# A 1444-key attention whose slots take in the value projection, the feed-forward and the norms behind it

## The reference

```python
z = self_attn(x, Wq1, Wk1, Wv1);            x = layer_norm(x + z, ln1_g, ln1_b)
z = cross_attn(x, context, Wq2, Wk2, Wv2);  x = layer_norm(x + z, ln2_g, ln2_b)
z = relu(x @ fc1_w + fc1_b) @ fc2_w + fc2_b
return layer_norm(x + z, ln3_g, ln3_b)
# the caller: x = x + tanh(g) * that, then x = x + tanh(g') * ffn(layernorm(x))
```

## Time and profile before

| | us |
|---|---|
| median of 3 runs | 2369.92 (2368.28 to 2373.06) |
| the profiled execution | 2365.66 |
| its span, first to last instruction | 2363.8 |
| cross-attention, first score matmul to last result copy | 134.8 to 402.2 |
| tail of stage A, to the first instruction of stage B | 402.2 to 624.4 |

### The profile page before, as it was taken

One profiled execution on the slowest core, in us unless ns is written; L12 is line 12 of the kernel. 1 busy time (PEld: TensorE's weight loads), 2 busy tenths in 40 slices (PEclk: granted clock), 3 DMA queues, 4 the chain that ended last, 5 costly groups with the idle time before them and its releaser, 6 DMA issues. The chain is left out here.

```text
span 2363.8 us, 43064 instructions
## 1 busy us (share of the span) xinstructions
PE 2000.1 (85%) x16906; PEld 1274.0 (54%) x16906; DVE 1588.6 (67%) x3726; ACT 1324.0 (56%) x2169; POOL 547.8 (23%) x476
## 2 busy tenths in 40 slices
PE   3779997465499999999999999999997788888997
PEld 2546665343255565555565565655654456565554
DVE  4835453688478778788788887887882466655554
ACT  3645554466236666666566666666665455544444
POOL 1410000454212222222221221222221232311122
PEclk9779998666579999999999999999999788877999
DMA  5026663000123232232232231332320100201431
GB/s 159 1 76 190 187 181 95 1 18 21 60 89 112 78 106 99 80 117 94 85 117 79 101 119 62 115 109 70 117 97 20 57 15 10 35 1 31 90 64 42
DMA packets 120022, 189.25 MB, mean 80 GB/s; under 512 B 36770, under 2 KB 94090, under 8 KB 118414
## 3 DMA queue, kind: packets, MB, share of 16 engines
q1 hardware_dynamic: 119822, 186.50, 25.6%
HBM read 103.33 MB, written 11.76 MB: 49 GB/s over the span
## 5 line engine op out<-in xcount | busy, mean ns | idle before, releaser
L1409 DVE TENSOR_REDUCE b_part_max<-psum 128x1 f32<-128x482 f32 (+3 forms) x1248 | 737.3, 650 | 187.6 <-PE psum L1286 173.5
L1199 ACT ACTIVATE b_PT<-psum 128x800 f32<-128x800 f32 x768 | 616.4, 836 | 386.0 <-PE psum L1305 379.6
L1286 PE MATMUL psum<-b_KH,b_QBD 64*128 64x482 f32 (+1 forms) x1152 | 421.4, 442 | 46.3 <-DVE b_part_max L1409 43.4
L1305 PE MATMUL psum<-b_QS,b_KS 64*128 64x200 f32 x3072 | 438.6, 288 | 0.5 <-ACT b_PT L1199 0.3
L1305 PEld LDWEIGHTS psum<-b_QS,b_KS 64*128 64x128 f32 x3072 | 339.6, 187 | 16.2 <-issue 11.8
L1321 PE MATMUL psum<-b_PT,b_V 128*32 128x200 f32 x6144 | 341.1, 339 | 0.6 <-ACT b_PT L1199 0.6
L1286 PEld LDWEIGHTS psum<-b_KH,b_QBD 64*128 64x128 f32 x1152 | 196.6, 188 | 198.0 <-DVE b_part_max L1409 118.6
L1122 POOL TENSOR_TENSOR b_KL<-b_KF,b_KH 128x1444 fp32r<-128x1444 f32 x32 | 106.9, 3340 | 691.9 <-PE psum L1305 669.7
L1321 PEld LDWEIGHTS psum<-b_PT,b_V 128*32 128x32 f32 x6144 | 159.9, 109 | 149.0 <-ACT b_PT L1199 82.3
L385 POOL TENSOR_TENSOR a_rs<-a_ve,a_half 100x4 f32<-100x4 f32 x48 | 50.0, 1041 | 419.5 <-DVE a_ve L758 419.4
L1709 ACT ACTIVATE c_HE<-psum,C 128x400 f32<-128x400 f32 x128 | 75.5, 594 | 94.7 <-PE psum L1925 90.1
(11 more groups left out here) (275 smaller groups left out, 3133.0 us busy)
## 6 DMA issues: line engine op xcount, KB each, us to landing
b_KS<-b_KH SPq DMA_DIRECT2D x64, 722.0 KB
a_CT<-in_ctxt SPq DMA_DIRECT2D x32, 722.0 KB, 4.2
b_CT<-in_ctxt SPq DMA_DIRECT2D x32, 722.0 KB, 4.3
b_KS<-b_KL SPq DMA_DIRECT2D x32, 722.0 KB
a_CN<-in_ctxn SPq DMA_DIRECT2D x32, 704.0 KB
att_scratch<-b_AO SPq DMA_DIRECT2D x32, 200.0 KB, 1.9
c_G<-gates_scratch SPq DMA_DIRECT2D x4, 1600.0 KB
c_KBD<-gates_scratch SPq DMA_DIRECT2D x4, 1600.0 KB
```

Source lines behind the costliest of these rows:

```text
L1199: nc.scalar.activation(PT[:, kt % 2, 2 * a:2 * a + 2, :], psum[:, 2 * a:2 * a + 2, 0:TG], ACT.Exp).then_inc(sem["pt_ready"], 1)
L1286: m = mm(bank(b, D, size), QBD[rows, j % 2, tile * D:(tile + 1) * D], KH[rows, j % 2, at_:at_ + size], start=True, stop=True)
L1305: m = mm(bank(p, D, 2 * T, (s % 2) * 2 * T), KS[rows, j % 2, s, kt * D:(kt + 1) * D], QS[rows, j % 2, s * 2 * T:(s + 1) * 2 * T], start=Tr ...
L1409: v.tensor_reduce(part_max[0:rows, q, c:c + 1], bank(b, rows, CHUNKS[c][1]), AX.X, ALU.max)\
```

## The change

- The front steps, `values2` to norm 4, are set in slots s. Slot s below 32 is sequence s of the attention; each tick of the tail stands for two more slots. Unit u does the step of lag k in slot 4 (u + 1) + k. Their PSUM bank is 5 in the attention and 1 in the tail.
- The scores are 512, 512 and 422 keys wide. Even sequences use banks 0, 1, 2, odd ones 2, 3, 4. The part in the shared bank 2 (part 2) is computed at the start of a slot, the two others of sequence m+2 between the second and third transposes of m; the wait for the key load stands in front of part 0.
- The mask of m+1 stands ahead of the whole weighing of m. The result copy on ACT stands behind the exponential of the next sequence.
- The residual is kept in `XIN` and the normalised rows in `Y`, for all units; `X` and its four buffers are gone. GpSimd computes `YB` ahead of the norm's shift.
- The tail has 11 ticks instead of 12. The loads of the context and their buffers are not touched.

```diff
+        def due(s, lag):
+            u, rest = divmod(s - lag, GROUP)
+            return u - 1 if rest == 0 and 1 <= u <= UNITS else None
+        def hop(s, rows, cols):
+            return bank(5 if s < BATCH else 1, rows, cols)
+        def chunks(m):
+            parts = [(c, 2 * (m % 2) + c, min(512, SPAD - 512 * c)) for c in range(3)]
+            return parts if m % 2 == 0 else parts[1:] + parts[:1]
...
# POOL
+            def front(s):
+                for lag, step in ((1, rstd(2)), (6, rstd(3)), (2, gain2), (7, gain3), (8, rstd(4))):
+                    if due(s, lag) is not None:
+                        step(due(s, lag))
...
# ACT
             for m in range(BATCH):
+                front_start(m)          # lag 4: turned2
                 keep(m, 0)
-                keep(m, 1)
                 if m + 1 < BATCH:
                     cut_row(m + 1)
+                keep(m, 1)
                 keep(m, 2)
-                act.wait_ge(sem["z2T_psum"], m + 1)
-                nc.scalar.copy(RT[:, m // GROUP, t.ts_(m % GROUP)], bank(7, D, T, TG)).then_inc(sem["z2T_ready"], 1)
+                front_middle(m)         # lag 4: rectify; 9, 2, 7: norms 4, 2, 3
                 if m + 1 < BATCH:
                     probabilities(m + 1)
+                result(m)
...
# PE
+            def score(m, part):
+                u, j = divmod(m, GROUP)
+                c, b, size = chunks(m)[part]
+                if part == 0:
+                    if m < 2:
+                        pe.wait_ge(sem["rT2_ready"], UNITS)
+                    else:
+                        pe.wait_ge(sem["e2_ready"], m - 1)
+                    pe.wait_ge(ct_loaded[m % 3], (m // 3 + 1) * 16)
+                if part == 2 and m:
+                    pe.wait_ge(sem["e2_ready"], m)
+                mm(bank(b, T, size), RT[:, u, t.ts_(j)], CT[:, m % 3, 512 * c:512 * c + size],
+                   start=True, stop=True).then_inc(sem["s2_psum"], 1)
...
             for m in range(BATCH):
+                pe.wait_ge(sem["e2_ready"], m + 1)
                 if m + 1 < BATCH:
-                    scores(m + 1)
-                pe.wait_ge(sem["e2_ready"], m + 1)
...
+                    score(m + 1, 2)
+                turn_keys(m, 0)
+                turn_keys(m, 1)
+                first_hop(m)            # lag 4: hidden
+                if m + 2 < BATCH:
+                    score(m + 2, 0)
+                    score(m + 2, 1)
+                turn_keys(m, 2)
+                if m + 1 < BATCH:
+                    cut(m + 1)
                 pe.wait_ge(cn_loaded[m % 3], (m // 3 + 1) * 32)
                 pe.wait_ge(sem["pT_ready"], m * 3 + 2)
                 weigh(m, 0, 8)
-                if m + 1 < BATCH:
-                    cut(m + 1)
                 pe.wait_ge(sem["pT_ready"], m * 3 + 3)
                 weigh(m, 8, KT).then_inc(sem["z2T_psum"], 1)
+                second_hop(m)           # lag 0: values2, 3: turn2, 5: outer
...
# PE, tail (ACT and DVE are interleaved with their front steps alike)
+            for tick in range(UNITS + 3):
+                s = BATCH + 2 * tick
+                at(turn4, 3)
+                first_hop(s)
+                at(down(0), 2)
+                at(down(1), 2)
+                second_hop(s)
+                at(down(2), 2)
+                at(down(3), 2)
+                first_hop(s + 1)
+                at(gate_up(2), 1)
+                at(gate_up(3), 1)
+                second_hop(s + 1)
+                at(turn3, 0)
+                at(gate_up(0), 0)
+                at(gate_up(1), 0)
...
# DVE
+            for m in range(BATCH):
+                if m + 1 < BATCH:
+                    link(count(m + 1, 2))
+                    length(m + 1)
+                front(m)                # lag 8: outcome, 1: residual2, 6: residual3
+                if m + 1 < BATCH:
+                    top(m + 1)
+                if m + 2 < BATCH:
+                    count(m + 2, 0)
+                    count(m + 2, 1)
```

More of the change, by code:

```diff
@@ L541, in inner_turned, with at @@
                 return step
[L543 to L549, removed]
+            for tick in range(UNITS + 3):
+                s = BATCH + 2 * tick
+                def at(step, lag):
+                    if 0 <= tick - lag < UNITS:
+                        step(tick - lag)
+                front_start(s)
+                at(quantised(0), 2)
+                at(quantised(1), 2)
+                at(inner_turned(0), 2)
+                front_middle(s)
+                at(quantised(2), 2)
+                at(inner_turned(1), 2)
+                at(quantised(3), 2)
+                at(inner_turned(2), 2)
+                front_start(s + 1)
+                at(turned4, 3)
+                at(inner_turned(3), 2)
+                at(gate(2), 1)
+                front_middle(s + 1)
+                at(gate(3), 1)
+                at(turned3, 0)
+                at(gate(0), 0)
+                at(normalise(5, lambda u: XIN[:, u], lambda u: U5[:, u % 2]), 2)
+                at(gate(1), 0)
         @block.tensor
@@ L639, in weigh, with values2, turn2 @@
                 return x_
-            scores(0)
+            def values2(s, u):
+                pe.wait_ge(sem["z2T_ready"], (u + 1) * GROUP)
+                if u:
+                    pe.wait_ge(sem["f1_ready"], u)
+                for j in range(GROUP):
+                    last = mm(hop_tokens(s)[:, j, :], RT[:, u, t.ts_(j)], w("v2"), start=True, stop=True)
+                last.then_inc(sem["z2_psum"], 1)
+            def turn2(s, u):
+                pe.wait_ge(sem["y2_ready"], u + 1)
+                if u:
+                    pe.wait_ge(var[3], u)
+                for j in range(GROUP):
+                    last = nc.tensor.transpose(hop(s, D, TG)[:, t.ts_(j)], Y[:, u, j, :], ident[0:T, 0:T])
+                last.then_inc(turned[2], 1)
@@ new lines, in hidden, with outer @@
+            def hidden(s, u):
+                pe.wait_ge(tokT[2], u + 1)
+                mm(hop(s, D, TG), w("fc1"), HT[:, u % 2, :], start=True, stop=True).then_inc(sem["f1_psum"], 1)
+            def outer(s, u):
+                pe.wait_ge(sem["f1_ready"], u + 1)
+                pe.wait_ge(var[2], min(u + 2, UNITS))
+                for j in range(GROUP):
+                    last = mm(hop_tokens(s)[:, j, :], HT2[:, u % 2, t.ts_(j)], w("fc2"), start=True, stop=True)
+                last.then_inc(sem["f2_psum"], 1)
@@ L642, in _, with first_hop, second_hop @@
+            def first_hop(s):
+                if due(s, 4) is not None:
+                    hidden(s, due(s, 4))
+            def second_hop(s):
+                if due(s, 0) is not None:
+                    values2(s, due(s, 0))
+                if due(s, 3) is not None:
+                    turn2(s, due(s, 3))
+                if due(s, 5) is not None:
+                    outer(s, due(s, 5))
+            for part in range(3):
+                score(0, part)
             cut(0)
+            score(1, 0)
@@ L643, in _ @@
+            score(1, 1)
             for m in range(BATCH):
+                pe.wait_ge(sem["e2_ready"], m + 1)
                 if m + 1 < BATCH:
-                    scores(m + 1)
-                pe.wait_ge(sem["e2_ready"], m + 1)
[L647 to L656, removed]
+                    score(m + 1, 2)
[8 more added lines that the diff above has]
+                    cut(m + 1)
@@ new lines, in front @@
+            def front(s):
+                for lag, step in ((8, outcome), (1, residual2), (6, residual3)):
+                    if due(s, lag) is not None:
+                        step(s, due(s, lag))
+            for part in range(3):
+                last = count(0, part)
+            link(last)
+            length(0)
+            top(0)
+            count(1, 0)
+            count(1, 1)
+            for m in range(BATCH):
+                if m + 1 < BATCH:
+                    link(count(m + 1, 2))
+                    length(m + 1)
+                front(m)
+                if m + 1 < BATCH:
[3 more added lines that the diff above has]
+                    count(m + 2, 1)
```

186 lines of the change are left out of this document (99 added, 87 removed).

## The result

The changed kernel took 2432.81 us (median of 4 runs, 2411.91 to 2441.46) against 2369.1 (4 runs). The ratio is 1.0254, 95% interval 1.0215 to 1.0293. The forecast was 2394, in a range to 2428: the sign and the closed cycle through the key load were right, the time was missed by 39 us and lies 5 us above the range.

A forecast was written before the change was run, and what follows sets the result against it. No single bound: attention a tight cycle, tail a chain of hand-overs; after the change the key load binds. Attention +65.9, clock +3.4, tail -45.1 make +24.2 us on the median 2369.92: 2394 us, range 2370 to 2428.

The forecast's parts named there:

- the sign: Whole kernel: the change makes it slower, chance 0.81, against faster 0.14 and same 0.05.
- the closed cycle through the key load: Attention: key load, scores, transposes, mask and weighing bind each other, 10.36 us per slot instead of 7.99; +65.9 us.
- The tail: Behind the attention: fewer front steps bring an earlier first result (33.5 us) and shorter ticks (11.6 us); -45.1 us.
- The tail's first part: Tail, from the attention's end to unit 0's result: 37 us instead of 70.5, 33.5 saved.
- The front steps: Inside the attention's slots: they cost nothing as long as the key load's wait covers them.
- Rival one: Attention: the key load does not bind, slots stay near 8.0 us, kernel 2331 us; chance 0.13.
- The cost that the prediction put beside this rival: Attention: GpSimd instructions could delay VectorE's small instruction after the maximum through shared ports, 15 us in all.
- The rival of a shorter load: Attention: load alone lands in some 2.6 us, slot 8.8, kernel near 2348; chance counted within rival one's 0.13.
- Between none and every second slot, I take two slots: +3.4 us.: Attention's clock: TensorE's idle stretch slows two slots, about 1.7 us lost in each.
- the third rival: Attention: the clock falls in most slots, 29 x 1.7 = 49 us instead of 3.4, kernel 2440; chance 0.11.

The follow-up runs named there:

- fill_hole: Changed kernel with 12 more transposes, results overwritten, in TensorE's hole ahead of the score matmul waiting for the keys; 2394.73 us, ratio 1.0101.
- after_mid_release: Changed kernel with the keys' load released after the first 16 of 24 weighing passes instead of the last; 2368.57 us, ratio 0.9993.
- early_keys: Changed kernel with the keys' load released by the scores of m-3 instead of its weighing, rows' load unchanged; 2332.03 us, ratio 0.9833.
- keys_alone: Changed kernel with the context rows' load issued only once the keys have landed; 2401.68 us, ratio 1.0146.
- before_early: Kernel before the change, with the keys' load released when the scores of the buffer's last user are done; 2368.22 us, ratio 0.9995.
- fill_short: As fill_hole on the changed kernel, but with 4 transposes instead of 12; 2403.8 us, ratio 1.0117.
- rows_first: Changed kernel with the two loads swapped, context rows first and keys behind them; 2567.49 us, ratio 1.0814.
- early_warm_tail: early_keys with identity transposes in the tail, 12 ahead of the quantised rows' wait and 6 ahead of norm 5's; 2336.32 us, ratio 0.9826.

## Why the prediction was right and where it failed

**Right, to its numbers.** The closed cycle through the key load: 10.36 us predicted, 10.0 to 10.5 measured in fill_hole, where the clock held, with each of its terms read again in the timeline; after_mid_release changed it by the amount that its sum gives, early_keys opened it. The tail: -42.9 against -45.1, both parts of it (32.8 of 33.5, and 10.1 of 11.6; one tick is 1.5 us longer). The tail's first part was summed with a small slip (9.6 and its four steps make 15.5, not 15.7), and its reading of the tail, no engine over 61% and a clock of 0.50, holds for the 20 us of the earlier trace rows alone: over the whole tail before, VectorE is busy 66% and the clock is 0.62. In the changed kernel the clock of the tail is 0.52, near the 0.50 that was assumed. The front steps: nothing seen under the cover of the load, a little over 1 us per unit without it. Rival one was priced at 2331 for the case that the load does not bind; early_keys is that case, 2332, with the last result copy 5.2 us later (priced 5.7). The cost that the prediction put beside this rival, GpSimd holding up the small instruction after the maximum, did not come: it took 0.15 us in each of the 32 slots, before, after and in early_keys.

**The rival of a shorter load** fell with keys_alone: worked out from the Trainium skill, DMA: Bandwidth & Descriptors, "Specifications", the load alone would land in some 2.6 us (the estimate of the prediction, from a bandwidth and a first byte, with nothing in it for the way from the last byte to the landing); alone it took 4.1. What the other 1.5 us are, no run here shows. The argument used against it there, that two loads share the engines, was wrong too: the second load behind it cost the first at most 0.1 us.

**Failed: "Between none and every second slot, I take two slots: +3.4 us."** Both factors were too small. 11 of 29 slots were hit, and a hit cost 3 us on average, up to 4.4, instead of 1.7. The 1.7 was taken from the weighing of the earlier trace rows alone, whose own difference is 5.58 - 3.23 = 2.35, and the two slots had no row behind them. In a closed cycle through TensorE, the scores, the transposes, the mask and the whole weighing are all on the path, and each is stretched. 36 us stand in the place of 3.4. In the profiled execution, where 41 us were missed (65.4 against 24.2), 32 are the attention's, 2 the tail's and 6 stage C's. fill_hole shows the term: with the stretch filled, the change takes 2394.7 us. That this is the forecast's own 2394 is in part luck, as the forecast had 3.4 us of clock in it. The argument against the third rival, that the hole is shorter than in the earlier trace rows and that full work stands on both sides, had weight for most slots but was taken for more than it could bear, and rival three (2440) was closer than the forecast. That closeness is luck too: it had too many hits (29) at too low a price (1.7), 49 us for 36. The rule that was put beside it, in the Trainium skill, TensorE: Matmul & The Clock Gate, "A second HAM failure mode: psum-queue depth-cycling", tells of short idle gaps between groups of matmuls in a bf16 kernel that cycles through PSUM banks. The trace agrees in kind, with gaps of another cause, a load: the clock swings here too, in 11 slots of 29. That every slot would be hit was the prediction's reading; the section gives no such count.

**The 6 us of stage C** in the profiled execution have the same code behind them. This was not tested by itself, but it needs no cause in the change: stage C took 524.0 us in the profiled execution of fill_hole, 530.8 in that of before_early, 531.8 in early_keys and 538.2 in after_mid_release and fill_short, with the clock of its second 100 us at 0.87 in the shortest.

## What to carry to other kernels

When work is moved to an earlier place in a loop, ask for each load in front of it what releases that load, and add the path from the release through the landing to the next release: if it comes out longer than the loop, the load binds, whatever it had to spare before. A buffer should be released by its own last reader, not by the last step of the iteration; here that one wait was the difference between +2.5% and -1.7%. Look also at what stands ahead of the load in its issuing engine's own order, which can be the true release, as in early_keys. And an idle stretch on TensorE is not priced by its length alone: price every TensorE step of the cycle at its duration at 1.2 GHz, and if the stretch can't be removed, see whether filling it holds the clock.

## What the runs showed that was not expected

- Wait for the keys per slot and slots hit, out of 29: 1.95 us and 11 (after), 1.73 and 3 (keys_alone), 1.16 and 3 (fill_short), 0.85 and 2 (after_mid_release), 0.4 and none (fill_hole). So no fall was seen where the stretch was nearly filled, but the length alone does not give the count: between the first two, nearly the same stretch gives very different counts, and 1.73 and 1.16 the same. Each is one profiled execution, and the changed kernel's own runs spread over 30 us (4 runs; those of the kernel before over 23 us in 23 runs).
- After a fall the clock can stay low through full work: TensorE was busy 10.00 of 10 us at 0.54 (262 to 272 us).
- The keys' load of 722 KB lands in 4.1 to 4.3 us (median) when no load was issued right ahead of it, with or without one behind it, but in 5.6 to 5.9 when it is issued 1.15 us behind the rows' load (rows_first, early_keys, before_early).
- Stage C's time moved by up to 17 us between profiled executions with the same code in it (524.0 in fill_hole, 541.1 in early_warm_tail).
